# Zero products between the links of the first batch's matrix chain, and two bias products moved ahead, in a fused attention and mixture-of-experts kernel on one Trainium2 core

## What is computed

```python
x = x + layernorm(attention(layernorm(x)))   # 16 heads of 8 channels, no softmax
x = x + layernorm(experts(layernorm(x)))     # 8 experts, top 2, and one shared expert
```

## Time and profile before

| What | us |
|---|---|
| median of 3 executions | 261.86 |
| lowest and highest of them | 260.1 and 265.44 |
| the profiled execution, its device time | 259.63 |
| its span (first to last instruction in the trace) | 257.7 |
| mean granted TensorE clock in it | 0.939 |

### The profile page before, as it was taken

How to read it: one execution, slowest core, us unless ns; L and a number is a source line. 1 busy time by engine, 2 the same in 40 slices (tenths; PEclk the granted TensorE clock), 3 DMA queues, 4 the chain that set the end, 5 groups by cost and what they waited for, 6 DMA issues and landing times.

```text
span 257.7 us, 5786 instructions
## 1 busy us (share of the span) xinstructions
PE 230.0 (89%) x1253; PEld 165.6 (64%) x1253; DVE 164.2 (64%) x736; ACT 135.5 (53%) x502; POOL 171.5 (67%) x216
## 2 busy tenths in 40 slices
PE   8879874969989849999999999999999999989980
PEld 3758663445454415344888888888888888879340
DVE  3964987649585948586975555655655556531595
ACT  2955692475535532555555555555555555511771
POOL 7963757886878787877776766666666666670630
PEclk9995997799968995999999999999999999999996
DMA  6797001110111111155123333332323233116973
GB/s 171 207 342 194 0 21 54 45 53 32 53 44 43 44 43 52 43 147 167 57 82 88 104 82 90 85 97 77 91 77 98 73 92 81 46 33 201 396 259 123
DMA packets 28314, 26.33 MB, mean 102 GB/s; under 512 B 7014, under 2 KB 22259, under 8 KB 28288
## 3 DMA queue, kind: packets, MB, share of 16 engines
q1 hardware_dynamic: 22448, 15.38, 21.3%
q0 software_dynamic: 4320, 8.53, 10.3%
q10 hardware_dynamic: 1520, 2.10, 2.3%
HBM read 14.77 MB, written 11.68 MB: 103 GB/s over the span
## 4 chain that ended last, share of the span: by engine, by line
PE 58%; POOL 12%; DVE 11%; issue 7%; ACT 6%; DMA 4%; POOLq 1%; ACTq 0%; DVEq 0%
PE bank L1310 13%; POOL expert_rows L521 8%; PE bank L1284 7%; PE bank L1285 6%; PE bank L1286 6%; PE bank L1302 6%; PE bank L1213 5%; PE bank L1265 3%; POOL rstd L513 3%; DMA xnT<-expert_results 2%; PE bank L1225 2%; PE bank L1186 2%; PE bank L1110 2%; DVE X L1081 2%; PE bank L1122 2%
## 5 line engine op out<-in xcount | busy, mean ns | idle before, releaser
L540 POOL DMA_INDIRECT expert_results<-eo,rowt x71 | 69.4, 978 | 34.5 <-issue 31.7
L521 POOL DMA_INDIRECT expert_rows<-src,slot x64 | 63.9, 998 | 22.1 <-issue 16.2
L1030 DVE TENSOR_TENSOR work<-work,bank 128x256 f32<-128x256 f32 x71 | 29.9, 421 | 41.4 <-ACT work L709 41.2
L709 ACT ACTIVATE work<-bank 128x256 f32<-128x256 f32 x71 | 27.3, 385 | 46.3 <-PE bank L1286 46.2
L1310 PE MATMUL bank<-down,work 128*128 x284 | 43.9, 277 | 0.0
L1310 PEld LDWEIGHTS bank<-down,work 128*128 128x128 f32 x284 | 37.2, 191 | 1.1 <-issue 0.2
L1284 PE MATMUL bank<-gu_hi,rh 128*128 x71 | 34.2, 482 | 0.0
L1213 PE MATMUL bank<-xT,gu_f 128*128 128x512 f32 x64 | 33.6, 654 | 0.2 <-ACT silT L620 0.2
L716 ACT ACTIVATE work<-bank 128x256 f32<-128x256 f32 x71 | 27.8, 392 | 0.7 <-PE bank L1302 0.7
L1285 PE MATMUL bank<-gu_lo,rh 128*128 x71 | 28.2, 397 | 0.0
L1286 PE MATMUL bank<-gu_hi,rl 128*128 x71 | 28.0, 394 | 0.0
(11 more groups left out here) (187 smaller groups left out, 431.7 us busy)
## 6 DMA issues: line engine op xcount, KB each, us to landing
rowt<-expert_rows SPq DMA_DIRECT2D x71, 66.0 KB, 1.9
X<-n_L_attn_in_sequence_bwc SPq DMA_DIRECT2D x8, 256.0 KB, 4.1
X<-expert_results SPq DMA_DIRECT2D x8, 256.0 KB, 6.7
xnT<-expert_results ACTq DMA_DIRECT2D x8, 256.0 KB, 7.4
out<-X SPq DMA_DIRECT2D x7, 256.0 KB, 2.7
expert_results<-eo,rowt POOLq DMA_INDIRECT x71, 2.3
gu_f<-in_L_ffn_gate_proj_w SPq DMA_DIRECT2D x1, 1024.0 KB, 6.6
gu_f<-in_L_ffn_up_proj_w SPq DMA_DIRECT2D x1, 1024.0 KB, 9.5
```

The costliest lines, as they stand in the source:

```text
L521: nc.gpsimd.indirect_dma_start(rows_d, bass.IndirectOffsetOnAxis(ap=slot[i % SRC][:, n // TOPK, n % TOPK:n % TOPK + 1], axis=0), src[i % S ...
L540: nc.gpsimd.indirect_dma_start(res_d, bass.IndirectOffsetOnAxis(ap=rowt[v][:, P:P + 1].bitcast(U32), axis=0), eo[v][:], None, bounds_check ...
L709: nc.scalar.activation(sgate[v % 2], gu_ps[v % 2][:, 0:M], ACT.Silu).then_inc(slot_silu, 1)
L1030: nc.vector.tensor_tensor(hid[v % 2], sgate[v % 2], gu_ps[v % 2][:, M:2 * M], ALU.mult).then_inc(slot_hid, 1)
```

## The change

Two calls of `warm_up(2)` are added: two products of zeros, 512 columns each, between link 1 and link 2, and two between `router_weights` and link 3. All zero products now write to bank 7 (bank 2 takes results of `metric_W` and `weights` at that time). The bias product is taken out of `attention` into a function of its own. For steps 0 and 1 it is issued earlier: that of step 0 behind link 3, that of step 1 behind link 4, both ahead of the wait for A_sb. For other steps it stays where it was. No instruction of another engine changes.

```diff
-        warm_ps = bank[2]
+        warm_ps = bank[7]
...
-            def attention(i):
-                b = i // QS
+            def attention_bias(i):
                 if i == 0:
                     pe.wait_ge(bias_ready, 2)
-                if i % QS == 0:
-                    pe.wait_ge(chain_sb[b], 5)
-                pe.wait_ge(xnT_done, i + 1)
...
                 if i >= 2:
                     pe.wait_ge(x1_done, (i - 1) * G)
                 mm(attn_ps[i][:, :], ones_r[:], bc(bias_2[:], 1, [2, G, C]), start=True, stop=False,
                    skip_group_check=True)
+
+            def attention(i):
+                b = i // QS
+
+                if i >= 2:
+                    attention_bias(i)
+                if i % QS == 0:
+                    pe.wait_ge(chain_sb[b], 5)
+                pe.wait_ge(xnT_done, i + 1)
...
             link(0, 1, S_sb[0][:], Wf)
+            warm_up(2)
             link(0, 2, Wf, T1[0][:])
             metric_W()
             pe.wait_ge(prep_sb, 2)
             router_weights()
+            warm_up(2)
             link(0, 3, Gm[0][:], mixT[:])
+            attention_bias(0)
             pe.wait_ge(LT_sb, 1)
             link(0, 4, LT[:], R_sb[0][:])
+            attention_bias(1)
             attention(0)
             attention(1)
             gram(4)
```

## The result

| | kernel before | changed kernel |
|---|---|---|
| median of 20 executions, us | 260.38 | 261.36 |
| lowest and highest, us | 258.22; 266.55 (and one of 751.98) | 260.12; 262.75 |
| profiled execution, us | 259.63 | 260.51 |
| its span, us | 257.7 | 258.6 |
| its mean granted clock | 0.939 | 0.934 |

The ratio of the changed kernel to the one before is 1.0059, with a 95% interval from 1.0033 to 1.0084: the change makes the kernel 0.6% slower, some 1.5 us. That the predicted 261.3 us is near the measured 261.36 is luck: it was put on a median of 3 executions (261.86) that 20 executions brought down to 260.38. The forecast was a small gain, and a small loss was measured. The ratio leaves out the disturbed executions of the kernel before, the six from 263.79 us up, of which the changed kernel has none (over all executions but the one of 751.98 both kernels have the mean 261.3).

A forecast was written before the change was run, and what follows sets the result against it. PE was taken to hold most of the chain (58%), with the clock falling after 18.2 us. Zeros 0, bias and clock -1.35, later fall +0.8 gave -0.55 us: median 261.86 to 261.3 us, range 258.6 to 264.5.

The forecast's parts named there:

- Zeros at no cost: Waits before links 2 and 3: each pair of zero products (0.41 us) fits the idle time, cost 0, bounds 0.2 us.
- The bias products hide: Waits before link 4 and for A_sb cover the moved bias products; attention(0) starts its A_sb products 0.69 us earlier, at 18.50.
- squares(0) 1.35 us earlier, bound by ACT: Behind attention(0): squares(0) starts at 19.95 instead of 21.30, since ACT normalises step 4 until 19.93.
- The fall comes later instead of going: Sparse PE stretch from 22 to 29 us: the clock falls there, about when gram(5) begins, instead of at 18.2.
- What it takes back, 0.8 us: gram(5) and logits at the lower clock: 1.24 + 0.3 - 0.7 of cover delays prefix(0), leaving 0.55 us at the first scatter.
- the rival of the full gain: Clock stays up through 29 us or falls under cover: the full 1.35 us is gained, 260.5 us; chance 0.24.
- That the rest travels on unchanged: From the first scatter onward: the 0.55 us gained there was taken as the change in total time.
- a rival with a chance of 0.13: Batch 1's chain and shared(0): PE arrives 0.45 us late, products stay slow, slots(2) 2.6 us later, 264.5 us; chance 0.13.
- It decides when POOL's wait before scatter(2) grows beyond 1.25 + 0.55 us: POOL ahead of scatter(2): the point from which the slower case by the second chain, 264.5 us, decides.
- The places where the clock is low: Page's clock slices: below full speed in three places, of which only the first lies near the change.
- The base: Median of the kernel before, taken as 261.86 us, with the profiled execution of 259.63 lying 2.2 us under it.
- The Trainium skill's rule: Only a long pause between matmul bursts lowers the clock: no fall at 18.2 or 28, so the full 1.35 us.

The follow-up runs named there:

- f3: Changed kernel plus 13 zero products where PE idles between 21 and 28 us; ratio to the kernel before 0.995, median 258.72 us.
- f0: The changed kernel measured again, beside the kernel before on one chip; ratio to the kernel before 1.0074, median 261.42 us.
- g1: Kernel before, without the change, plus 13 and 19 zero products between 21 and 46 us; ratio to the kernel before 1.0034, median 260.79 us.
- f1: Changed kernel without the zero products between the links, bias products still moved ahead; ratio to the kernel before 1.0009, median 260.9 us.
- g3: Changed kernel with its four zero products but the bias products where they were; ratio to the kernel before 1.0029, median 261.25 us.
- g4: Changed kernel plus 19 zero products around logits(1) and batch 1's chain, none added at 21 to 28 us; ratio to the kernel before 0.996, median 258.59 us.
- e2: Changed kernel with its zero products but the bias products where they were, on the first chip (kernel before 297.2 us); ratio to the kernel before 0.9999.
- f4: Changed kernel plus 13 zero products at 21 to 28 us and 19 up to batch 1's last link; ratio to the kernel before 0.9907, median 257.74 us.
- g2: Changed kernel plus the 13 and 19 zero products, and 13 more ahead of rows_T(6); ratio to the kernel before 0.9904, median 256.98 us.
- e3: Changed kernel plus 13 zero products between 21 and 28 us, on the first chip (kernel before 297.2 us); ratio to the kernel before 0.9863.
- e4: Changed kernel plus 13 zero products at 21 to 28 us and 19 up to batch 1's last link, on the first chip; ratio to the kernel before 0.9971.
- e1: Changed kernel without the zero products between the links, bias products moved ahead, on the first chip (kernel before 297.2 us); ratio to the kernel before 0.9979.

## Why the prediction was wrong, by its own steps

- **Zeros at no cost: right.** Links 2, 3 and 4 keep their distances within 0.02 us.
- **The bias products hide: right.** The products of attention(0) start 0.44 us behind the bias of step 1, at +3.00 from link 2, against +3.73 before: 0.73 us, predicted 0.69.
- **squares(0) 1.35 us earlier, bound by ACT: right**, and a little better: 1.46 us. ACT starts it 0.09 us ahead of the end that its row gives for the four normalised tiles (18.01 + 1.63).
- **The fall comes later instead of going: right in kind**, at 26.3 instead of the expected 28, that is, within rows_T(0) and ahead of logits(0), not at gram(5).
- **What it takes back, 0.8 us: the step that failed first.** The terms were 1.24 for gram(5), 0.3 for the logits, less 0.7 of cover. gram(5)'s tiles are 0.64 us apart (30.34 to 30.98), so this term stands. logits(0) took 1.87 us instead of 1.06, 0.8 and not 0.3, and rows_T(0), which I had left at the full clock, 1.25 instead of 1.10. That makes 1.24 + 0.8 + 0.15 - 0.7 = 1.5 us, and 1.42 are measured at prefix(0). Nothing is left at the first scatter: 34.76 is the old 35.04 less the 0.29 us of the earlier start. With the later fall covered (f3) the first scatter is 1.48 us earlier than before, counted from link 2: this is what the rival of the full gain had priced at 1.35.
- **That the rest travels on unchanged: the step that gave the wrong sign.** I summed the forecast at the first scatter, put what the second batch's chain and shared(0) would add at nothing, and left it to a rival with a chance of 0.13. That rival happened. PE reached prefix(1) 0.24 us later (42.41 against 42.17; 0.53 us from link 2, where the rival had 0.45), and in f0 1.24 us later. The second low stretch began 2.2 us earlier, while PE was in logits(1), and ended 1.2 us later, at 50.2, and shared(0) took 5.33 us and in f0 6.09 instead of 4.84, that is 0.49 and 1.25 us more where the rival had 2.15. Its price was 2.6 us at scatter(2); measured were 0.68 in the profiled execution and 2.45 in f0 (62.29 - 59.84). Over many executions the loss is 1.5 and 1.9 us (0.59% and 0.74%), between half and three quarters of what the rival had.
- **It decides when POOL's wait before scatter(2) grows beyond 1.25 + 0.55 us: right for the change, but no rule.** The wait is 2.10 and 3.47 us in the change, with a loss. But f3 gains with 2.21 us, because both POOL and PE get there earlier, and g1 gains nothing with 0.20, because POOL gets there late. The start of scatter(2) is the better measure: with it at 57.4 to 59.2 the span is below that of the kernel before, with it at 60.1 to 62.3 above.
- **The places where the clock is low.** The prediction read three in the page's slices. There are four (18, 42, 73 and 97 us), and of them the second, which I held to lie away from the change, is where the sign was made.
- **The base.** Three executions gave the median 261.86, twenty 260.38. The profiled execution at 259.63 was nearer to the truth than I made it when I called it 2.2 us under the median.
- **The Trainium skill's rule** ("TensorE: Matmul & The Clock Gate", section "Why this matters for your kernels"), by which only a long pause between bursts takes the clock down, would have given the full gain. The trace disagrees: the clock fell at 26.3 with idle times of 1.62 and 1.15 us ahead of it. It also fell at 18.2 in the kernel before with none over 0.46 us. In f3, where such short waits are filled, the clock stayed up.

What stays open: how the loss divides between the zeros and the moved bias products; how often the late fall comes without a cover (it is in the profiles of the change, f0, f1, g3 and g4, and not in that of e2); and why f4, whose last slot result is 2.5 us before that of the kernel before (226.7 against 229.2), has a span only 1.0 us shorter. In the profiled executions of f4 and g2 the stage behind the slots takes 30.0 and 29.8 us, in those of the other kernels on chips of this speed 28.5 to 29.1.

## What to carry to other kernels

Keeping the clock up at one sparse place moves work forward and can widen the next one: here PE had no idle time ahead of attention(2) before, and 1.62 us after the change. Ask what PE does in the stretch after the one that is repaired, and fill all of them up to the point where another engine is the bound, or measure whether a single one pays. A forecast is to be summed at the last place where the moved engine and the bounding one meet (here scatter(2)), not at the first. Filler belongs only in front of waits that are there in every execution: where PE can be late, it delays the chain, as in g1, whose first scatter came 1.3 us later from link 2 than in the kernel before.

## What the runs showed of the hardware

- Products of zeros count: with 13 of them between 21 and 28 us the granted clock was 1.00 there in all six profiles (e3, e4, f3, f4, g2 and, once it was back up, g1), while it fell to 0.50 between 25.3 and 28.5 us in five profiles without them (the change, f0, f1, g3, g4) and stayed up in one (e2). With 19 more up to the last link of batch 1 it was 1.00 there too (f4, g4, g1, g2), but not on the chip with the stalls: in e4 it fell at 43.4, inside a wait of PE of 3.3 us for ACT's copy of link 1.
- Executions of one kernel differ in where the clock falls, and the differences are as large as the effect of the change: the same program had its first fall at 27.1 us in f1 and at 19.4 in e1, and the change was low from 26.3 to 33.1 us in one profile and from 25.4 to 35.7 in another (f0). The executions of f4 spread over 2.1 us (256.68 to 258.77), those of the kernel before that the ratio counts on the same chip over 3.3 us (258.0 to 261.34).
- Chips differ by more than any of this: the kernel before took 297.2 us on one and 260.0 on two others.
